# Attention queries: projected turned, copied out by ScalarE, halves exchanged by a lane shuffle, products and sum on GpSimd

## What is computed

```
q  = layernorm(x) @ w_q.T              # 16 heads of 32
kv = layernorm(x) @ w_kv.T             # one head for k, one for v, 32 each
q  = q*cos*scale + rotate_half(q)*sin*scale     # rotate_half: (-second half, first half) of the 32
k  = the same with 1/scale
out = softmax(causal(q @ k.T)) @ v ;  x = x + out @ w_proj.T + b_proj
```

## Time and profile before

| | |
|---|---|
| median of 3 runs | 2854.09 us (2853.02 to 2855.83) |
| the profiled execution | 2851.07 us, its span 2849.3 us |
| PE busy | 2749.1 us (96%), weight loads 2210.9 (78%) |
| VectorE (DVE) busy | 1846.5 us (65%) |
| ScalarE (ACT) busy | 1144.0 us (40%) |
| GpSimd (POOL) busy | 317.6 us (11%) |
| DMA | 156.12 MB, mean 55 GB/s |

### The profile page before, as it was taken

One profiled execution on the slowest core, in us unless ns is written; L12 is line 12 of the kernel. 1 busy time (PEld: TensorE's weight loads), 2 busy tenths in 40 slices (PEclk: granted clock), 3 DMA queues, 4 the chain that ended last, 5 costly groups with the idle time before them and its releaser, 6 DMA issues. The chain is left out here.

```text
span 2849.3 us, 42018 instructions
## 1 busy us (share of the span) xinstructions
PE 2749.1 (96%) x15648; PEld 2210.9 (78%) x15648; DVE 1846.5 (65%) x3487; ACT 1144.0 (40%) x2432; POOL 317.6 (11%) x347
## 2 busy tenths in 40 slices
PE   7999999999999996899999997999999999999998
PEld 5888888888888884667777765888888888888887
DVE  5667656766676665666666665656766666676655
ACT  3323333323233321777777774332333333333331
POOL 0000000000000002455554521000000000000000
PEclk9999999999999997999999998999999999999999
DMA  3210311121121103000000002211121122203100
GB/s 117 99 51 23 125 45 44 61 89 45 45 81 64 48 1 113 1 9 31 27 27 31 16 16 107 101 45 44 60 89 45 48 80 78 69 23 104 45 15 30
DMA packets 65022, 156.12 MB, mean 55 GB/s; under 512 B 6864, under 2 KB 6992, under 8 KB 64592
## 3 DMA queue, kind: packets, MB, share of 16 engines
q1 hardware_dynamic: 64848, 153.77, 16.0%
HBM read 128.58 MB, written 25.17 MB: 54 GB/s over the span
## 5 line engine op out<-in xcount | busy, mean ns | idle before, releaser
L350 PE MATMUL bank<-xnt_h,wgu_h 128*128 128x512 f32 x2048 | 803.2, 392 | 10.3 <-issue 7.4
L350 PE MATMUL bank<-xnt_h,wgu_l 128*128 128x512 f32 x2048 | 798.9, 390 | 0.0
L350 PE MATMUL bank<-xnt_l,wgu_h 128*128 128x512 f32 x2048 | 798.5, 390 | 0.0
L507 DVE TENSOR_TENSOR h<-bank,sg 128x512 f32<-128x512 f32 x256 | 176.9, 691 | 600.1 <-PE bank L350 586.0
L350 PEld LDWEIGHTS bank<-xnt_h,wgu_h 128*128 128x128 f32 x2048 | 385.6, 188 | 90.8 <-issue 8.6
L350 PEld LDWEIGHTS bank<-xnt_h,wgu_l 128*128 128x128 f32 x2048 | 385.4, 188 | 80.6
L350 PEld LDWEIGHTS bank<-xnt_l,wgu_h 128*128 128x128 f32 x2048 | 385.8, 188 | 79.3
L446 ACT ACTIVATE mag<-h 128x512 f32<-128x512 f32 x256 | 162.2, 634 | 702.3 <-DVE h L507 702.3
L369 PE MATMUL bank<-wd_h,hs_h 128*128 128x512 f32 x1024 | 400.0, 391 | 9.1 <-DVE hs_l L542 9.1
L369 PE MATMUL bank<-wd_l,hs_h 128*128 128x512 f32 x1024 | 399.5, 390 | 0.0
L369 PE MATMUL bank<-wd_h,hs_l 128*128 128x512 f32 x1024 | 399.4, 390 | 0.0
(11 more groups left out here) (114 smaller groups left out, 3273.7 us busy)
## 6 DMA issues: line engine op xcount, KB each, us to landing
raw_gu<-in_w_gu SPq DMA_DIRECT2D x128, 512.0 KB, 4.9
raw_d<-in_w_d SPq DMA_DIRECT2D x128, 256.0 KB, 2.6
x_mid<-x_sb SPq DMA_DIRECT2D x64, 256.0 KB, 2.0
x_sb<-in_x SPq DMA_DIRECT2D x32, 256.0 KB, 4.9
x_sb<-x_mid SPq DMA_DIRECT2D x8, 1024.0 KB, 5.5
x_sb<-x_mid SPq DMA_DIRECT2D x32, 256.0 KB, 4.8
out<-x_sb SPq DMA_DIRECT2D x32, 256.0 KB, 2.1
probs<-in_w_q SPq DMA_DIRECT2D x1, 1024.0 KB, 5.4
```

Of the source, the lines that this page charges most:

```text
L350: last = pe.matmul(ps, w[:, r, kind, k], xs[:, b, k], start=(i == 0), stop=(i == 3 * KD - 1))
L507: v.tensor_tensor(h[:, r], bank[UP + r % 2][:, :], sg[:, r % 2], ALU.mult).then_inc(h_done, 1)
```

## The change

- The operands of the query projection change places: the weights of one group of heads stand still and all 512 tokens stream. The output of one turn is 128 features (four heads of 32) x 512 tokens, which is the layout that `turn_q` made. `turn_q`, its steps and its copies are gone.
- ScalarE's `drain_q` copies the projection from PSUM to `qt`, in steps 1, 2, 5 and 6, between two of its exponentials.
- VectorE's `copy_q` becomes `swap_q`: a stream shuffle over partitions, SBUF to SBUF, `qt` to `qtmp`, in which each of the 32 lanes of a head takes the one 16 away.
- GpSimd multiplies `qt` with the cosine table in place, `qtmp` with the sine table, and adds: three instructions of 128x512.
- For batch 0 the same functions are used, so VectorE no longer multiplies there.
- `qt` and `qtmp` have two buffers; the tables for q and k are two tensors, loaded by two DMAs (q: 128 x 2 x 512, k: 128 x 4 x 2 x 32 floats) instead of one.

```
-            TURN_X, TURN_KV, TURN_K, TURN_Q = {11: 0, 12: 1, 13: 2, 14: 3}, 1, 4, {10: 0, 11: 1, 12: 2, 13: 3}
+            TURN_X, TURN_KV, TURN_K = {11: 0, 12: 1, 13: 2, 14: 3}, 1, 4
-            ROTATE = {2: 0, 3: 1, 6: 2, 7: 3}
+            FINISH = {2: 0, 3: 1, 6: 2, 7: 3}
+            SWAPPED = [(d + HALF) % HD for d in range(HD)]
...
+                    def finish_q(B, hg):
+                        n = B * NHG + hg
+                        q, tmp = qt[:, B % 2, hg], qtmp[:, n % 2]
+                        g.wait_ge(q_swapped, n + 1)
+                        g.tensor_tensor(q, q, rot_q[:, 0], ALU.mult).then_inc(q_scaled, 1)
+                        g.tensor_tensor(tmp, tmp, rot_q[:, 1], ALU.mult).then_inc(q_scaled, 1)
+                        g.wait_ge(q_scaled, (n + 1) * 2)
+                        g.tensor_tensor(q, q, tmp, ALU.add).then_inc(q_finished, 1)
...
+                    def project_q(B, hg):
+                        ps = take_turn(("q", B, hg), q_copied, B * NHG + hg + 1)
+                        cols = slice(hg * P, (hg + 1) * P)
                         for k in range(KD):
+                            for n, (w, x) in enumerate(((wq_h, xnt_h), (wq_l, xnt_h), (wq_h, xnt_l))):
+                                last = pe.matmul(ps[:, :], w[:, k, cols], x[:, 0, k], start=(k == n == 0),
...
                         if k % TT == 0:
-                            pe.wait_ge(qt_done, B * NHG + hg + 1)
+                            pe.wait_ge(q_finished, B * NHG + hg + 1)
...
                     def drain_q(B, hg):
+                        a.wait_ge(q_done, B * NHG + hg + 1)
+                        if hg == 0 and B >= 2:
+                            a.wait_ge(score_done, (B - 1) * UNITS)
+                        a.copy(qt[:, B % 2, hg], bank_of["q", B, hg][:, :]).then_inc(q_copied, 1)
...
                         exps(K + 1, 3)
+                        if nxt < BATCHES and PROJECT.get(k, ("", 0))[0] == "q":
+                            drain_q(nxt, PROJECT[k][1])
...
+                    def swap_q(B, hg):
+                        n = B * NHG + hg
+                        v.wait_ge(q_copied, n + 1)
+                        if n >= 2:
+                            v.wait_ge(q_finished, n - 1)
+                        v.stream_shuffle(qtmp[:, n % 2], qt[:, B % 2, hg], SWAPPED).then_inc(q_swapped, 1)
...
+                    swap_q(0, 0)
                     keys(0)
                     for t in range(1, TT):
-                        rotate_first_q(t)
+                        swap_q(0, t)
                         stat(1, t - 1)
```

More of the change, by code:

```diff
@@ L28, with macaron_kernel @@
 MASKED = 3.0e38
-def macaron_kernel(nc, x_in, w_gu, w_d, w_q, w_kv, w_p, b_p, rotary, out):
+def macaron_kernel(nc, x_in, w_gu, w_d, w_q, w_kv, w_p, b_p, rotary_q, rotary_k, out):
     BATCHES, S, D = x_in.shape
@@ L108, in macaron_kernel @@
     wkv_l = place("wkv_l", [P, KD, 2 * HD], F32R)
-    rot = place("rot", [P, TT, 4, HD], F32)
+    rot_q = place("rot_q", [P, 2, S], F32)
+    rot_k = place("rot_k", [P, TT, 2, HD], F32)
     bias = place("bias", [P, D], F32)
@@ L191, in macaron_kernel @@
         q_copied = sem("q_copied")
[L192 removed]
+        q_swapped = sem("q_swapped")
+        q_scaled = sem("q_scaled")
         q_finished = sem("q_finished")
[L194 to L195 removed]
         score_done = sem("score_done")
@@ L835, in step @@
                         if nxt < BATCHES:
-                            if k in ROTATE:
-                                rotate_q(nxt, ROTATE[k])
+                            if k in FINISH:
+                                finish_q(nxt, FINISH[k])
                             if k == 1:
@@ L944, in scores @@
                             rows = slice(s * HD, (s + 1) * HD)
-                            last = pe.matmul(bank[SCORES + s][:, 0:width(i)], qt[rows, hg, i * P:(i + 1) * P],
+                            last = pe.matmul(bank[SCORES + s][:, 0:width(i)], qt[rows, B % 2, hg, i * P:(i + 1) * P],
                                              kt[rows, B % 2, 0:width(i)], start=True, stop=True)
@@ L1128, in _ @@
                     drain_kv(0)
+                    drain_q(0, 0)
                     drain_kvtok(0)
+                    drain_q(0, 1)
+                    drain_q(0, 2)
                     drain_k(0)
+                    drain_q(0, 3)
                     a.wait_ge(aw_loaded[3], 16)
@@ L1177, in keys @@
                         v.tensor_copy(kwide[:, :, :, :], krot[:, 0].unsqueeze(2).to_broadcast([P, TT, HG, HD])).then_inc(k_step, 1)
[L1179 to L1189, removed]
-                        sin = rot[:, t, 1].unsqueeze(1).to_broadcast([P, HEADS, HD])
-                        rotate(heads_of(bank_of["q", 0, t][:, :]), heads_of(qrot[:, t]), heads_of(qraw[:, t % 2]), cos, sin, q_rotated)
+                    def swap_q(B, hg):
[4 more added lines that the diff above has]
+                        v.stream_shuffle(qtmp[:, n % 2], qt[:, B % 2, hg], SWAPPED).then_inc(q_swapped, 1)
                     def mask_scores(K, heads):
@@ L1348, with by_token, by_dimension @@
     sign = _np.concatenate([-_np.ones(HD // 2, f), _np.ones(HD // 2, f)])
-    tables = _np.stack([-_np.cos(ang) * sc / f(HD), -_np.sin(ang) * sc * sign / f(HD),
-                        _np.cos(ang) / sc, _np.sin(ang) * sign / sc], axis=1).astype(f)
-    tables = _np.ascontiguousarray(tables.reshape(S // 128, 128, 4, HD).transpose(1, 0, 2, 3))
+    def by_token(*two):
+        return _np.ascontiguousarray(_np.stack(two, axis=1).astype(f).reshape(S // 128, 128, 2, HD).transpose(1, 0, 2, 3))
+    def by_dimension(*two):
+        return _np.ascontiguousarray(_np.stack([_np.tile(a.T, (128 // HD, 1)) for a in two], axis=1).astype(f))
+    tables_q = by_dimension(-_np.cos(ang) * sc / f(HD), -_np.sin(ang) * sc * sign / f(HD))
+    tables_k = by_token(_np.cos(ang) / sc, _np.sin(ang) * sign / sc)
     arrays = {
@@ L1360 @@
         "b_p": _np.ascontiguousarray(_np.asarray(inputs["L0_attn_b_proj"]).reshape(1, D)),
-        "rotary": tables,
+        "rotary_q": tables_q,
+        "rotary_k": tables_k,
     }
```

70 lines of the change are left out of this document (11 added, 59 removed).

## The result

The changed kernel takes 2844.66 us (median of 7 runs, 2842.25 to 2846.96), the kernel before 2855.83 us in the same comparison (7 runs). The ratio is 0.9965, with a 95% interval from 0.9954 to 0.9976: the change makes the kernel 7 to 13 us faster, 10 us by the middle. I had forecast 3.4 us with the sign of a gain, and given "no change that can be told apart" most of the chance. The time lies inside the range, 0.2 us above its lower end.

What follows compares the result with a forecast made beforehand. PE was taken as the bound, busy 75.14 of 77.18 us a batch. Terms -12.25 (turning), +3.0 (ScalarE) and +5.8 (start) gave -3.4 us: 2847.7 on the profiled execution, 2850.7 on the median's scale; range 2844.5 to 2858.5.

Steps and rivals of the forecast that it cites:

- no change that can be told apart: Whole kernel: time within about 0.2%, 5.7 us, of the kernel before; chance 0.60.
- The turning of the queries, batches 1 to 6: PE, steps 10 to 13: removed transposes gain 1.95 us in each of batches 1 to 5, 1.3 in batch 6.
- the 0.79 of step 11: Step 11: without the query turn and its PSUM bank wait, the weighting starts earlier; gain 0.79 us a batch.
- the floor of step 12: Step 12: cannot fall below 3.05 us, as step 8 with its wait for VectorE's masking; gain 0.28 us.
- ScalarE's new wait in step 2: Step 2: moved copy delays the keys-and-values copy whose bank PE needs; 0.42 us, 3.0 us over seven batches.
- The rival of ScalarE's queue at all four places: Copy delays PE at four places a batch, 0.42 us each: 11.8 instead of 3.0 us, 2859.5 us; chance 0.16.
- VectorE: Loop: the shuffle replacing the PSUM copy takes 0.7 us plus 0.1 for the lane table, hidden, 0 us.
- 1.4 us a shuffle: Dear shuffle rival: +1.4 us over seven batches and 2 in the start, 2854 us in all; chance 0.10.
- GpSimd ahead of the loop: Before the loop: GpSimd's longer queue and collisions with VectorE make deviations 6.3 us late; net cost 5.8 us.
- Batch 0: Batch 0, removed query turns: 1.2 us of gain taken from a possible 1.5.
- the start is cheaper: Ahead of the loop: lateness absorbed, 5.8 us become 0, 2844.9 us; chance 0.24, together with a larger gain.
- my own, -6 to -1 us: Whole kernel: the forecast of -3.4 us with its near variants; chance 0.50.

Runs made afterwards that it cites:

- e5_keys_first: Changed kernel with batch 0's keys rotated on VectorE ahead of the first shuffle instead of behind it; 2846.29 us, ratio 0.9979 to the kernel before.
- b_busy: Kernel before with four more GpSimd instructions of 128x512 ahead of batch 1's deviations; 2857.67 us, ratio 1.0014 to the kernel before.
- b_fill: Kernel before with twelve idle products, whose result nobody reads, in step 9 of batch 0; 2852.19 us, ratio 0.9995 to the kernel before.
- e3_turns_kept: Changed kernel with the query transposes and their copies put back in steps 10 to 13, results unused; 2857.96 us, ratio 1.0014 to the kernel before.
- e12_both: Changed kernel with ScalarE's copy behind the exponentials in steps 1 and 5, and batch 1's deviations ahead of the third query group; 2841.03 us, ratio 0.9961.
- e7_shuffle_twice: Changed kernel with each lane shuffle done twice in a row; 2850.69 us, ratio 0.9991 to the kernel before.
- e12_fill: As e12_both, plus idle products on PE: eight ahead of the loop, twelve in step 9 of batch 0; 2835.16 us, ratio 0.9942 to the kernel before.
- a2: Changed kernel once more, unaltered, for a second trace; 2843.9 us, ratio 0.9964 to the kernel before.
- e2_deviations_early: Changed kernel with batch 1's deviations made on GpSimd after the second of four query groups, not the fourth; 2841.89 us, ratio 0.9959 to the kernel before.

## Why the prediction was right or wrong

- **The turning of the queries, batches 1 to 6: right.** Forecast 9.75 + 1.3 = 11.05 us; kept against removed in the same kernel is 11.15. The steps came out at the hundredth, the 0.79 of step 11 and the floor of step 12 among them.
- **ScalarE's new wait in step 2: right.** Forecast 0.42 us and 3.0 in all; measured 0.43 and, taken away, 3.04. Steps 5 and 6 cost nothing, as said. The rival of ScalarE's queue at all four places didn't come.
- **VectorE: right.** The shuffle takes 0.74 us and the loading of the lane table 0.01 (0.7 and 0.1 taken). The estimate from the Trainium skill ("VectorE: DVE Perf Modes", the perf-mode tiers), 0.6 us, is short by a fifth. Its rule, the slow mode alone, fits what the rows show: 0.74 us against 0.43 for the plain copy that writes as much. For 1.4 us a shuffle I had 0.2 us a batch, from step 6; the doubled shuffle cost 0.27, but in steps 3 and 7.
- **GpSimd ahead of the loop: right in place, 0.8 and 1.4 us too dear.** Forecast 6.3 us later deviations and 5.8 net. Measured 5.5 on the means of the pairs (5.9 and 5.0 by trace), 5.3 at the first turned probabilities and 4.4 at scores 3. The collisions were there, three of them, and the rule in "SBUF — State Buffer", section on the two sides, agrees with the trace: 1.32 against 0.22 us, and back to 0.22 in e5_keys_first. What I left out is that PE's clock comes back sooner after the later start: between the first turned probabilities and scores 3 lie 6.0 and 5.3 us in the traces of before and 5.0 and 4.6 in those of the changed kernel. The clock from the projection of step 0 to scores 3 is 0.51 and 0.62 in the former, 0.66 and 0.74 in the latter. Since the clock differs from trace to trace too, that this comes of the later start is not shown; b_busy, as late, has 6.0 us.
- **Batch 0: this term was mis-sized, and it made most of the miss.** I took 1.2 us of gain less 0.4 for ScalarE. The traces give 3.1 in the first pair and 4.4 in the second, so the 1.2 measured 3.5 and 4.8. Steps 10 to 12 at full clock give 1.3 of it (b_fill against the changed kernel: 2.99 to 2.73, 5.19 to 4.40, 3.33 to 3.05), as I had. Two things were missing. First, step 14, which my sum leaves out, is 0.63 us shorter (4.09 to 3.46). In the kernel before, PE's second block of probabilities there waits for the copy of the turned x; in the changed kernel it starts together with the first:

```profile
1212.27 0.66 PE L954 MATMUL bank<-ident,probs 128*128 128x128 f32 x4
1213.09 1.14 PE L954 MATMUL bank<-ident,probs 128*128 128x128 f32 x8 [0.17 <-ACT xt_raw L1072]
```

```profile
1214.94 1.53 PE L927 MATMUL bank<-ident,probs 128*128 128x128 f32 x12
```

  One turn fewer in each step shifts the rotation of the three banks, so that the third block, and not the second, gets the bank that is freed late. I followed the rotation for step 11 and not for batch 0. Second, step 10's 4.54 us in the trace of before, which I put down in part to ScalarE, are the clock: at full clock it takes 2.99 (b_fill, e3_turns_kept). That is 1.6 us in the first trace of before, and 2.8 in the second (5.35 in step 10, and 5.65 instead of 5.20 in step 11), which the changed kernel lost in neither. The runs do not show that the change brings this part: the clock stays up in e3_turns_kept, with the old turns, and falls in two traces without them (e12_both, e7_shuffle_twice).
- **The sum.** Forecast for the loop -9.25 us, measured -11.4 and -12.7 (the first and the second traces); for the start +5.8, measured +4.4 by the means. In all -7.7 in the attention phase by the means of the traces (-6.1 and -9.3 by the two pairs), against -3.4; of the 4.3 us between them 2.9 are batch 0 and 1.4 the start. The whole spans differ by -6.5 and -9.5 us. The timed difference is -10 with an interval from -13 to -7. What lies between is partly the choice of execution (the first trace of before is 3 us below the median of its three runs); whether it is all of it, the two traces of each kernel cannot say.
- **The chances.** The time, 2844.66 us, is that of the rival "the start is cheaper" (2844.9), but by luck: the start did cost 4.4 us, and the rest came in batch 0. It fell in the case that had 0.24, and my own, -6 to -1 us, had 0.50. The range holds it by 0.2 us. The cases were right and their bounds too narrow on the gain's side: I let the two clock-bound places stand as they were in a single trace.

## What to carry to other kernels

Price a removed instruction on a saturated engine from the distance of starts, step by step, with the waits that its buffer makes for others; that gave the steps of batches 1 to 6 to the hundredth. A copy moved to another engine costs by what queues behind it there, so put it after the work that is ready, not before. And look which stretches of the one trace ran at a lower clock before taking any duration from them: a chain of waits, a start or a first batch may be 1 to 2 us shorter or longer in the next execution.

## What the runs showed of the hardware

- Nearly the same wait, 2.3 to 2.6 us, ahead of the same step lowers the tensor engine's clock in some executions and not in others (5 of 11 traces without the filler), at 1.2 to 2.4 us in that step. By the Trainium skill, "TensorE: Matmul & The Clock Gate", part on the clock gate, the point at which the clock rises at the start of work varies from run to run; the traces show the like for its fall. With idle products in the wait of 3.68 us ahead of the loop the clock behind it is 1.00 (e12_fill, one trace), where the twelve traces without them have 0.51 to 0.74. For the twelve in step 9 the two traces with them are too few to tell.
- The clock falls in batch 7 as well, in steps 2 to 3 or 6 to 7, in eleven of the thirteen traces. The two without the fall (e7_shuffle_twice and e12_fill) have 49.0 us there instead of 50.2 to 50.3.
- The last feed-forward block, with the same code, takes 1070.3 to 1072.7 us in the traces, and between the ends of this range the clock is the difference. Its first 5 us in the first trace of before and in a2 (us, PE, weights, VectorE, ScalarE, GpSimd, clock):

```profile
1778.91:1783.91 5.00, 5.00 (x16) 4.06 (x17) 3.79 (x5) 2.60 (x3) 1.04 (x1) 0.71 0.55 165
```

```profile
1769.16:1774.16 5.00, 5.00 (x12) 3.98 (x13) 3.79 (x5) 2.00 (x2) 1.04 (x1) 0.50 0.51 169
```

  The first 60 products take 14.1 us in the one and 15.7 in the other. PE also waits 4.5 us for the last down projections; from there to the end it is 15.7 and 16.4 us, the clock of the first 4 us being 0.62 and 0.50. Together that is 2.2 of the 2.4 us.
- A collision goes both ways: where VectorE cuts the output weights, 2.51 us with two operands in SBUF, a GpSimd instruction that elsewhere takes 1.27 us took 3.20 (e2_deviations_early):

```profile
1136.11 2.51 DVE L1126 TENSOR_TENSOR wp_l<-raw_p,wp_h 128x2048 fp32r<-128x2048 f32 x1
1136.55 3.20 POOL L787 TENSOR_TENSOR qt<-qt,qtmp 128x512 f32<-128x512 f32 x1
```
